# The last 772 columns of each softmax row are masked by a second scoring in PSUM instead of by VectorE

## The reference, cut to what matters

```python
Q = (x_text @ Wq).reshape(Bb, Tt, H, DH)
K = (x_vision @ Wk).reshape(Bb, Gg, H, DH)
scores = jnp.einsum('bthd,bghd->bhtg', Q, K) / np.sqrt(DH).astype(np.float32)
topv, topi = jax.lax.top_k(scores, K_TOP)          # K_TOP = 32
probs = jax.nn.softmax(topv, axis=-1)
attn = jnp.zeros_like(scores).at[bi, hi, ti, topi].set(probs)
attn_mean = attn.mean(axis=1)                      # over the 4 heads
c_t = jnp.einsum('btg,bgd->btd', attn_mean, V)
```

## Time and profile before

| | us |
|---|---|
| median of 3 runs | 1981.69 |
| lowest and highest run | 1971.29, 1982.04 |
| profiled execution | 1984.06 |
| its span in the profile | 1982.3 |
| first attention, from the first score to the last transposes | about 201 to 832 |

### The profile page before, as it was taken

One profiled execution on the slowest core, in us unless ns is written; L12 is line 12 of the kernel. 1 busy time (PEld: TensorE's weight loads), 2 busy tenths in 40 slices (PEclk: granted clock), 3 DMA queues, 4 the chain that ended last, 5 costly groups with the idle time before them and its releaser, 6 DMA issues. The chain is left out here.

```text
span 1982.3 us, 22568 instructions
## 1 busy us (share of the span) xinstructions
PE 1588.0 (80%) x8229; PEld 609.4 (31%) x8229; DVE 856.1 (43%) x2286; ACT 1375.4 (69%) x1374; POOL 177.7 (9%) x153
## 2 busy tenths in 40 slices
PE   4357978889889887573645999999999999996996
PEld 3236424455455444441310111111111111113342
DVE  5734699999999999463320000000000000003223
ACT  3471677878778777310315999999999999992432
POOL 2753011121021021000000000000000000000000
PEclk7566999999899998686766999999999999997998
DMA  2122086797797797476011000610060000003000
GB/s 84 54 93 98 11 159 152 172 215 161 158 215 158 161 221 188 101 126 92 3 26 22 1 1 1 57 14 1 10 62 1 1 1 1 1 1 92 0 0 11
DMA packets 90018, 145.01 MB, mean 73 GB/s; under 512 B 46783, under 2 KB 59544, under 8 KB 88976
## 3 DMA queue, kind: packets, MB, share of 16 engines
q0 software_dynamic: 13472, 75.53, 19.0%
q1 hardware_dynamic: 76000, 67.14, 15.6%
q10 hardware_dynamic: 432, 0.85, 0.1%
HBM read 54.10 MB, written 13.99 MB: 34 GB/s over the span
## 5 line engine op out<-in xcount | busy, mean ns | idle before, releaser
L1814 ACT ACTIVATE ex<-ps 128x1536 f32<-128x1536 f32 x536 | 722.3, 1498 | 5.9 <-PE ps L1768 5.8
L788 PE MATMUL ps<-K,qst 128*128 128x512 f32 (+1 forms) x832 | 392.2, 602 | 35.6 <-ACT srow L858 22.7
L1783 PE MATMUL ps<-ex,V 128*9 128x512 f32 x3200 | 419.5, 596 | 0.5 <-ACT ex L1814 0.4
L1768 PE MATMUL ps<-Q,K 52*128 52x512 bf16 (+1 forms) x1632 | 322.5, 385 | 72.0 <-PEq L106 36.7
L1824 DVE COPY o<-ps 9x512 f32<-9x512 f32 x32 | 22.0, 687 | 745.2 <-PE ps L1787 744.4
L989 DVE MAX8 cand<-srow 128x8 f32<-128x200 f32 (+1 forms) x1024 | 328.6, 382 | 8.1 <-ACT srow L858 8.1
L949 DVE SCALAR_TENSOR_TENSOR both<-srow,top,both 128x1536 f32<-128x1536 f32 (+1 forms) x128 | 242.6, 1895 | 27.1 <-ACT both L875 27.1
L858 ACT COPY srow<-ps 128x1024 f32<-128x1024 f32 (+1 forms) x224 | 205.2, 924 | 47.8 <-PE ps L788 47.4
L875 ACT ACTIVATE both<-srow,shift 128x1536 f32<-128x1536 f32 (+1 forms) x128 | 209.6, 1640 | 23.5 <-DMA both<-both 22.4
L1768 PEld LDWEIGHTS ps<-Q,K 52*128 52x128 bf16 (+1 forms) x1632 | 60.5, 93 | 480.7 <-ACT ex L1814 433.8
L788 PEld LDWEIGHTS ps<-K,qst 128*128 128x128 f32 x832 | 150.0, 197 | 171.3 <-issue 115.6
(11 more groups left out here) (310 smaller groups left out, 1112.7 us busy)
## 6 DMA issues: line engine op xcount, KB each, us to landing
both<-both POOLq DMA_DIRECT2D x69, 768.0 KB, 8.8
v_ring<-v_rows SPq DMA_DIRECT2D x84, 256.0 KB, 6.0
both<-both POOLq DMA_DIRECT2D x23, 898.0 KB, 13.2
K<-k_parts SPq DMA_DIRECT2D x48, 204.0 KB
k_parts<-kl SPq DMA_DIRECT2D x12, 384.0 KB, 2.5
V<-v_rows SPq DMA_DIRECT2D x4, 900.0 KB, 30.5
v_rows<-v1g SPq DMA_DIRECT2D x12, 288.0 KB, 3.0
srow<-v_rows SPq DMA_DIRECT2D x1, 3200.0 KB, 18.2
```

The lines of the kernel that those rows point to most:

```text
L788: last = M.matmul(ps[:, BANK_OF[item] + b, 0:c1 - c0], qst[:, h, :], K0[:, c0:c1], start=True, stop=True)
L1768: last = M.matmul(out, K1[rows_, quad % 2, hh // 2, keys], Q1[rows_, 4 * quad + hh, tb * TB:(tb + 1) * TB], start=True, stop=True, tile_po ...
L1783: last = M.matmul(out, V1[:, quad % 2, g, VW * j:VW * j + VW], ex1[:, slot(w, 4 * g + j), :], start=g == 0, stop=False, tile_position=(0, ...
L1814: C.activation(ex1[:, s:s + NBANK, :], ps[:, b:b + NBANK, :], ACT.Exp)\
```

## The change

The chunks become 2048, 2048, 1536 and 772 columns. VectorE masks the first three, after pieces 25, 28 and 31. The fourth (`LOW`) is no longer masked by VectorE, except in the last item. Instead:

- VectorE multiplies the 32nd largest by 2^100 (`steep`, one column);
- ScalarE writes `penalty` = Relu(steep - 2^100 x score), in bf16, 772 columns: zero where the score is kept, huge elsewhere (`penalties`, right behind `exp_shift`);
- TensorE scores these 772 columns a second time into two banks of the ring and subtracts the penalty in the same accumulation, as a bf16 matmul with minus the identity (`scores_again`, right behind group 5 of the item two later);
- ScalarE takes the exp from PSUM into `both` (`exps_again`, where the fourth `exps` was, behind the evacuation of group 5).

GpSimd issues the fourth chunk's add behind `exps_again`, ahead of the next item's first three. `queries` loads an item's query two items ahead instead of four, since the second scoring still reads the old one.

```diff
-    CH_OF = [3, 3, 3, 4]
+    CH_OF = [4, 4, 3, 2]
+    STEEP = 2.0 ** 100
+    AGAIN_AT = 5
-    MASK_AFTER = {24: 0, 27: 1, 29: 2, 31: 3}
+    MASK_AFTER = {25: 0, 28: 1, 31: 2}
...
+        if k // NGRP >= 2 and k % NGRP == AGAIN_AT:
+            ITEMS.append(("again", k // NGRP - 2))
...
+                def scores_again(n):
+
+                    item = ITEM_AT["again", n]
+                    pe.wait_ge(S("evac"), FREE_AT[item])
+                    pe.wait_ge(S("penalized"), n + 1)
+                    for b, c0 in enumerate(range(CUTS[LOW], G, 512)):
+                        c1 = min(c0 + 512, G)
+                        out = ps[:, BANK_OF[item] + b, 0:c1 - c0]
+                        M.matmul(out, qst[:, n % H0, :], K0[:, c0:c1], start=True, stop=False)
+                        last = M.matmul(out, minus[:, :], penalty[:, c0 - CUTS[LOW]:c1 - CUTS[LOW]], start=False, stop=True)
+                    last.then_inc(S("rescored"), 1)
...
                         scores(n, g)
+                        if n >= 2 and g == AGAIN_AT:
+                            scores_again(n - 2)
...
+                def penalties(n):
+
+                    s = n % SLOTS
+                    act.wait_ge(S("steep_ready"), n + 1)
+                    if n:
+                        act.wait_ge(S("rescored"), n)
+                    C.activation(penalty[:, :], srow[:, s, chunk(LOW)], ACT.Relu, scale=-STEEP, bias=steep[:, s:s + 1])\
+                        .then_inc(S("penalized"), 1)
+
+                def exps_again(n):
+
+                    s, b = n % SLOTS, BANK_OF[ITEM_AT["again", n]]
+                    home_free(act, n, LOW)
+                    act.wait_ge(S("rescored"), n + 1)
+                    C.activation(both[:, home(n), chunk(LOW)],
+                                 ps[:, b:b + GBANK, :].rearrange("p a b -> p (a b)")[:, 0:G - CUTS[LOW]], ACT.Exp,
+                                 bias=shift[:, s:s + 1]).then_inc(S("evac"), 1)
...
                                 exp_shift(older)
+                                penalties(older)
                                 exps(older, 0)
...
-                            if g == 5:
-                                exps(older, 3)
+                            if g == AGAIN_AT:
+                                exps_again(older)
...
-                    if n + H0 < NI:
-                        queries(n + H0)
+                    if n >= 2 and n + 2 < NI:
+                        queries(n + 2)
...
+                        if r == 3:
+                            V.tensor_scalar(steep[:, s:s + 1], top40[:, s, TOPK - 1:TOPK], STEEP, None, ALU.mult)\
+                                .then_inc(S("steep_ready"), 1)
...
                 for n in range(LAST):
-                    for c in range(NCH):
+                    if n:
+                        add(n - 1, LOW)
+                    for c in range(LOW):
                         add(n, c)
+                add(LAST - 1, LOW)
```

More of the change, by code:

```diff
@@ L691, in program @@
     for n, (kind, k) in enumerate(ITEMS):
-        size = min(GBANK, NBK - (k % NGRP) * GBANK) if kind == "scores" else 1
+        size = min(GBANK, NBK - (k % NGRP) * GBANK) if kind == "scores" else GBANK if kind == "again" else 1
         if at + size > RING:
@@ L744, in kept_by @@
         def kept_by(n, c):
-            return n * NCH + c + 1
+            return n * LOW + c + 1
         STEPS = 10
```

26 lines of the change are left out of this document (21 added, 5 removed).

## The result

The change makes the kernel slower: **2061.77 us** (2060.44 to 2068.56) against 1980.68 us of the kernel before on the same chip, a ratio of 1.0417 [1.0374, 1.046]. The forecast was 1970. By the medians that is 81 us more. The profiled executions took 2060.44 us, with a span of 2058.6, and 1984.06 before, 76 us apart, so the two traces can be read for the difference.

A forecast was written before the change was run, and what follows sets the result against it. VectorE bounds the kernel (18.06 us an item), with TensorE next and binding after the change at 17.75. Gains of 5.2 and 7.8 less 1.2 make 11.8 us, so 1970 us against a median of 1981.69; range 1952 to 1990.

The forecast's parts named there:

- VectorE's saving: VectorE's masks: larger and fewer masks less one `steep` save net 0.87 us an item, a beat of 17.19 us.
- ScalarE's prices: ScalarE: penalty of 772 columns adds 0.84 us an item; the four exps cost the same, also from PSUM.
- Covered, with 1.1 us to spare: ScalarE's work with the penalty, 16.1 us an item, fits within the beat of 17.19.
- The second scoring: TensorE: rescoring and subtracting 772 columns costs 1.63 us an item, bounds 1.57 and 1.88, weight loads hidden.
- the estimate of 2.27 us: TensorE's second scoring if six weight loads were not hidden, 0.64 us more; weighed from the skill page, not adopted.
- The queue behind the second scoring: TensorE's ring order after group 5: items needing group 4's evacuation take 18.3 us after the pick, against a beat of 17.75.
- the first kind gets that back, as it starts 2.8 us earlier. So I leave 17.75: Items whose second scoring needs only group 3's evacuation make up the longer chain, leaving the beat at 17.75 us.
- my sum: TensorE's need per tile of four items: 66.8 us of work plus 4.2 of DMA waits, 71.0 us.
- the ring takes it all: Rival: every item has the 18.3 us chain, beat stays 18.06 once transposes run; 1978 us, chance 0.13.
- The values' DMA: TensorE's waits for the values' loads stay at 4.2 us a tile, since bytes and the adds' sum are unchanged.
- more late items: Rival: a slow-clock wait of TensorE costs VectorE 2.65 us once a tile, 16 in all; 1986 us, chance 0.12.
- The slower case: Rival: TensorE's idle time is unusable, so each item with transposes grows by 1.63 us; 2018 us, chance 0.08.

The follow-up runs named there:

- experiment 13: Changed kernel with three values buffers; second scoring done in group 5's banks, no ring entry, last 772 columns unmasked: 1953.5 us, ratio 0.9888.
- experiment 9: Kernel before with three buffers for the values' loads instead of two and three `meanT` buffers instead of four: 1974.13 us, ratio 0.9968.
- experiment 8: Changed kernel with the penalty computed for 4 columns only, the rest zero, so the last 772 columns are hardly masked: 2051.22 us, ratio 1.0356.
- experiment 6: Changed kernel with three buffers for the values' loads instead of two and three `meanT` buffers instead of four: 1992.33 us, ratio 1.0065.
- 11: Changed kernel with three values buffers and the second scoring cut to 4 columns a bank, ring entry kept: 1988.91 us, ratio 1.0029.
- 12: Changed kernel with three values buffers and a ring of six PSUM banks instead of seven: 2002.29 us, ratio 1.0112.
- experiment 3: Changed kernel with the second scoring cut to 4 columns a bank, ring entry, waits and penalties kept, last 772 columns unmasked: 2010.15 us, ratio 1.0141.
- 16: Changed kernel with two values buffers; second scoring's work in group 5's banks, no ring entry, last 772 columns unmasked: 2033.36 us, ratio 1.0279.
- experiment 1: Kernel before with the new chunks alone (2048, 2048, 1536, 772), all masked by VectorE: 1973.49 us, ratio 0.9973.
- 7: Changed kernel with the penalty behind the first exp instead of ahead of it: 2049.43 us, ratio 1.0347.
- experiment 2: Kernel before with 772 columns of group 5 scored twice into the same banks, no ring entry, no ScalarE work: 1983.57 us, ratio 1.0042.
- experiments 4: Changed kernel without the values' loads after the first two of the stage, stale values used: 1990.06 us, ratio 1.0062.

## Why the prediction was wrong

**VectorE's saving: right.** A mask of 2048 takes 544.31 - 542.04 = 2.27 us (forecast 2.25). There are four intervals ahead of the first transposes and not "some 6": they belong to item 6, just behind the `exp_shift` of item 4. In the change these are 16.39, 16.73, 17.19 and 19.57 (forecast 17.19), in experiment 13 the third and the next two are 17.18 or 17.19. In experiment 13 the 31 intervals sum to 552.3 against 577.0, 24.7 less, but the third slot alone takes off 9.8 (experiment 9), which leaves 14.9 where 25.8 was the whole of the saving. So the saving is shown in single masks and beats, and never came in whole.

**ScalarE's prices: right.** Penalty 0.84, exp from PSUM 0.80. "Covered, with 1.1 us to spare" was wrong: taking the penalty away shortens the ordinary beat by 0.64 (experiment 8). The sum of ScalarE's work fits the beat, but it lies in a chain that others wait for, and the prediction itself had said that place matters more than sum.

**The second scoring: right.** 1.72 us for 1.63, in experiment 13 498.48 - 496.75 = 1.73. Both stand behind a wait of TensorE; where it comes straight from group 5, as at 424.94 in experiment 6, the six instructions take 1.62 to 1.63, and the 0.1 is the first instruction's behind the wait. A bf16 matmul of 512 columns takes 0.22 from start to start and 260 columns 0.12, so 0.34 for the 0.33 taken. The rule of the Trainium skill ("TensorE: Matmul & The Clock Gate", The mechanism) that was weighed, that a weight load overlaps only if it goes to other row groups, with the estimate of 2.27 us, is contradicted here too. The same section also lets a load run ahead into a background weight buffer, and with that the measurement agrees.

**The queue behind the second scoring: the second failed step.** The chain itself was right in kind. Of the kind that needs the evacuation of group 4, the scoring starts 8.1 us after the pick where I had 7.5, and the next pick is taken up 11.3 after that where I had 9.9 + 0.89 = 10.8. The 1.1 us more are, as I read them, a copy of `meanT` on ScalarE that I had left out (500.37 - 499.91 = 0.46 in the trace of the change) and some 0.2 at each handing over between the two engines. So the beats are 19.35 and 20.0 and not 18.3. And "**the first kind gets that back, as it starts 2.8 us earlier. So I leave 17.75**" failed. It does start earlier, 4.8 and 6.1 us after the pick and not 8.1 and 8.6; but then the ring, with an entry of two banks more an item, stops TensorE at the next item's groups for ScalarE's evacuations (0.78 at 429.31 and 467.67), and the beat is 18.2 and 18.3. Nothing is given back in a ring: an item cannot start ahead of ScalarE's. Four items take 75.9 us where my sum said 71.0, although TensorE is busy only 65.93 of 72 in this kernel, and although the 4.2 us of DMA waits in my sum are gone with the third slot. I had added TensorE's work and its DMA waits, and left out that it and ScalarE wait for each other. The experiments fix the cause: the work away and the entry kept gives 3 to 7 us (11), the entry away and the work kept gives 36 (13). What in the entry costs, the two banks or ScalarE's wait for the second scoring, they do not tell apart; a bank less costs 10 to 15 us more (12). Of the rivals, "the ring takes it all" had the right mechanism, with 18.06 as its price; what it costs is a beat of 18.98 on the mean (75.9 / 4).

**The values' DMA: the first failed step, and the larger.** "**The change moves no byte of these, and the adds keep their sum (6404 columns) with larger first pieces, so I keep 4.2.**" The bytes are the same, but not what stands ahead of them. A load is issued when an earlier values group is summed, some 3 us before it is wanted, and a tile's last load, of 192 KB, lands close to the last add issued clearly ahead of it: in the change that is the second of two adds of 1024 KB. The nine kernels with two slots that load the values have 54 such loads in their first six tiles:

| what is issued less than 8 us ahead of the load | places | issue to landing | landing behind that add |
|---|---|---|---|
| no add | 6 | 3.3 to 4.2 | 0.5, behind one issued 10.6 to 11.1 us ahead |
| the last add, at most 0.4 us ahead (two of them in experiments 3 and 16) | 12 | 2.9 to 5.8 | 3.7 to 7.4 ahead of it |
| one add of 768 KB, 0.8 to 2.3 us ahead | 11 | 4.7 to 7.5 | 0.2 to 0.5 |
| one add of 1024 KB, 1.5 and 1.3 us ahead (experiment 1) | 2 | 7.0 and 8.1 | 0.4 and 0.2 |
| two adds of 1024 KB, the second 0.6 to 3.0 us ahead (the change, 7, 8, 16) | 23 | 7.4 to 11.5 | 1.5 ahead of it to 1.6 behind |

With the third slot a load may be issued when no add is under way, and then takes 2.5 to 2.7 us (256 KB, at 542.8 and 548.6 in experiment 6). The DMA engines are full around the late item's load, with 219 GB/s at a share of 1.00 from 529 to 548, as they were at 1.03. Six late items cost 8.4 to 10.2 us each above the same item with a third slot (28.4 to 30.3 against 20.0), 54 us, and the rest of the 69 lies in the neighbours (up to 21.5 and 22.74 where 18.34 stands) and in the last item.

The rival "more late items" was closest: once a tile, after a wait, at half clock. It was priced 6 x 2.65 = 16 from the earlier trace rows, where TensorE had waited 2.13 us; here it waits 5.89, and all of it comes through, since TensorE's lag is not absorbed by an engine that is ahead of the others. The price of a late item was read from a place where VectorE hid most of it; so the range, with 1990 at its upper end, missed. The granted clock over 555 to 569 is 0.79 (0.50 from 556 to 560), in the window

```profile
555.00:569.00 14.00, 13.50 (x31) 6.63 (x32) 2.63 (x6) 7.34 (x11) 0.00 (x0) 0.79 0.43 98
```

and 12 instructions took 7.16 us for 12 x 0.43 = 5.2; the values group ahead of them took 557.01 - 555.17 = 1.84, and 0.95 for the same six instructions in experiment 6. Together 2.9 us of the 8.9 that the item loses are the clock's, behind TensorE's idleness of 5.89. The Trainium skill ("TensorE: Matmul & The Clock Gate", A second HAM failure mode: psum-queue depth-cycling) speaks of gaps between groups as a cause of such swings. The trace agrees in that the fall of each late item stands behind a wait; experiment 6, with waits of 0.3 to 1.3 us in every item, keeps a clock of 1.00, so short gaps of that kind don't do it here.

**The slower case** at 0.08 had another mechanism, the work itself, and it isn't that (experiment 2). The outcome was slower for reasons that stood among the rivals with too small a price. The work does matter by way of the loads: with two slots 52 us go with it (experiment 3).

**What is open.** That the late load makes the item late is shown by experiments 4 and 6. Why it is late in the change has two parts. The adds come sooner relative to the load: the first of the item stands 4.9 us ahead of it in the change and at most 1.6 us ahead of it in the kernel before (541.40 and 546.26, 507.53 and 509.12), and in experiment 3, without the work, it is still 3.7 us. And TensorE's 1.7 us of work ask for the load later, 1.6 us behind the second add and not 0.4 (experiment 3), which is the step from 4.9 to 8.8 us. Neither the chunks alone (1) nor the work alone (2) brings a second add ahead of the load, and the ring entry isn't needed for it (16). That the adds come sooner because of VectorE's shorter beat is argued and not shown. Nor is the landing with the add a rule for every load: a load of 256 KB issued 1.2 us behind an add of 898, with others under way, landed 2.4 us ahead of it (338.76 in experiment 2). Nor is it settled whether the DMA engines are a bound of their own. In the three items of four that are added, 3.28 MB of adds and 0.83 MB of loads are 228 GB/s at a beat of 18.06 and 239 at 17.2, where the full windows read here show 219 and 223; over four items it is less, 180 GB/s at a share of 0.81 before and 188 at 0.84 in experiment 13. Smaller adds with all else of the change kept, `MSLOTS` of 3 by itself, and banks for the second scoring outside the ring that still deliver its result, weren't tried.

## What to carry to other kernels

Adding up an engine's work and its old waits tells the new beat only while another engine is well ahead; when the change takes away that engine's lead, walk every ring and buffer through two whole items, and price a late transfer by what it holds up, not by what was seen while it was covered. A buffer that is reloaded just in time can need one slot more when something else shares the DMA engines: it cost one slot of `meanT` here and was worth 69 us in the one kernel and 6 in the other. And a step that occupies banks of a ring costs by how it orders the two engines (36 us here), even when its instructions are nearly free (3 to 7 us). A step can be nearly free in one kernel and not in another: the same 1.7 us of work were worth 52 us where they moved a load behind an add.

## What was not expected of the hardware

- **Where a small load is issued against a large add of another engine decides when it lands.** Issued at most 0.4 us behind an add, 192 KB landed after 2.9 to 5.8 us, well ahead of that add, in 12 places; issued 0.6 to 3.0 us behind it, in 36 places, they landed close to it, 1.5 us ahead to 1.6 behind, after 4.7 to 7.5 us behind 768 KB, 7.0 and 8.1 behind 1024 and 7.4 to 11.5 behind twice 1024. The Trainium skill ("DMA: Bandwidth & Descriptors", Anatomy of one DMA) has a fixed cost and a rate for a single transfer issued by GpSimd; worked out from that page 256 KB would take about 2.6 us and 192 KB about 2.5, an estimate. The loads here are issued by SyncE; the trace agrees where no add is under way (2.5 to 2.7 us for 256 KB), and not behind adds.
- **The bf16 matmul inside the float32 accumulation** takes 497.93 - 497.71 = 0.22 us for 512 columns and 0.12 for 260. All six instructions take 1.62 to 1.63 us in an unbroken stream and 1.72 to 1.73 behind a wait, 0.1 us more at the first of them; the float32 ones are otherwise not slower than in their own stream.
- **Short waits of TensorE in every item left the clock alone**: 1.00 in every window read of experiment 6, with waits of 0.3 to 1.3 us, and 0.50 from 556 to 560 in the change, behind one of 5.89.
